# Causal attention in 32-row groups: scores and row maxima of one head each, from unmasked keys, with all masks on VectorE

## What is computed

```python
qkv = x @ W_qkv.T + b_qkv                     # x: layer norm of 4 x 1024 x 128
Q, K, V = ...                                 # each split into 16 heads of 8 channels
scores = jnp.einsum('bqhd,bkhd->bhqk', Q, K)
scores = jnp.where(causal, scores, -jnp.inf)
probs = jax.nn.softmax(scores / sqrt(hd), axis=-1)
out = jnp.einsum('bkhd,bhqk->bqhd', V, probs)
return out.reshape(B, S, H) @ W_o.T + b_o
```

## Time and profile before

| | |
|---|---|
| median of three runs | 2132.38 us |
| profiled execution | 2132.39 us, its span 2130.6 us |
| PE busy | 1859.3 us, 87% |
| DVE, ACT, POOL busy | 72%, 62%, 52% |
| scores L2207 | 768 matmuls, 226.3 us busy |
| maxima L2277, reductions L2419, masked maxima L2415 | 250.5, 230.9 and 157.3 us busy |
| values L2224 | 1536 matmuls, 164.1 us busy |
| head-mask products L2124 on POOL | 30, 108.0 us busy |

### The profile page before, as it was taken

The page is one execution under the profiler, slowest core; times in us unless marked ns, Lnnn a source line. Parts: engine busy times, 40 slices in busy tenths (PEclk is TensorE's granted clock), DMA queues, the critical chain, the costliest instruction groups (busy, mean ns, idle before and its releaser), DMA issues. The chain is left out here.

```text
span 2130.6 us, 30582 instructions
## 1 busy us (share of the span) xinstructions
PE 1859.3 (87%) x9650; PEld 1284.4 (60%) x9650; DVE 1538.1 (72%) x4002; ACT 1318.5 (62%) x2323; POOL 1114.9 (52%) x1073
## 2 busy tenths in 40 slices
PE   6887699997999966673799979999999999988999
PEld 3554588876788632332588845555555555547887
DVE  6996877756677679998677667766766766736775
ACT  3443388862788744442688845665666666557887
POOL 1110388862788822320688944543543543327888
PEclk8998799999899987876799989999999999998999
DMA  3000254400543300000333300000000000004442
GB/s 103 6 5 5 75 207 160 181 34 1 203 171 150 116 1 1 1 0 0 150 150 150 150 0 1 1 1 1 1 1 1 1 1 1 1 1 164 189 191 95
DMA packets 38803, 142.28 MB, mean 67 GB/s; under 512 B 6962, under 2 KB 18930, under 8 KB 26355
## 3 DMA queue, kind: packets, MB, share of 16 engines
q1 hardware_dynamic: 36336, 139.55, 16.9%
q10 hardware_dynamic: 2306, 0.78, 0.2%
HBM read 136.38 MB, written 3.93 MB: 66 GB/s over the span
## 5 line engine op out<-in xcount | busy, mean ns | idle before, releaser
L2327 ACT ACTIVATE soft_prob<-psum 128x1024 f32<-128x1024 f32 (+3 forms) x384 | 302.7, 813 | 205.5 <-PE psum L2207 203.9
L2419 DVE TENSOR_REDUCE soft_mx<-psum 128x1 f32<-128x512 f32 (+2 forms) x352 | 230.9, 687 | 116.5 <-PE psum L2277 79.4
L2277 PE MATMUL psum<-soft_own,soft_stack 128*128 128x512 f32 (+3 forms) x768 | 250.5, 378 | 24.1 <-DVE soft_mx L2415 10.5
L2207 PE MATMUL psum<-soft_stack,soft_own 128*128 128x512 f32 (+3 forms) x768 | 226.3, 378 | 2.7 <-POOL soft_stack L2184 2.2
L163 POOL TENSOR_TENSOR norm_rstd<-norm_mv,s_const_minus_half 128x4 f32<-128x4 f32 x64 | 65.5, 1023 | 275.9 <-DVE norm_mv L158 269.6
L2190 POOL TENSOR_SCALAR_AFFINE_SELECT soft_prob<-soft_prob 128x256 f32<-128x256 f32 x256 | 103.0, 409 | 203.6 <-ACT soft_prob L2327 200.8
L2207 PEld LDWEIGHTS psum<-soft_stack,soft_own 128*128 128x128 f32 x768 | 125.7, 190 | 133.3 <-issue 78.3
L2415 DVE CUSTOM_DVE_ANT_0 psum<-psum,s_soft_sel 128x384 f32<-128x384 f32 (+1 forms) x256 | 157.3, 639 | 66.2 <-PE psum L2277 65.5
L2277 PEld LDWEIGHTS psum<-soft_own,soft_stack 128*128 128x128 f32 x768 | 140.7, 194 | 92.5 <-DVE soft_mx L2419 42.8
L934 POOL TENSOR_TENSOR ffn0b_h_low<-ffn0b_t,ffn0b_h_high 128x512 fp32r<-128x512 f32 x128 | 162.3, 1297 | 29.9 <-ACT ffn0b_t L1067 29.8
L934 POOL TENSOR_TENSOR ffn1a_h_low<-ffn1a_t,ffn1a_h_high 128x512 fp32r<-128x512 f32 x128 | 162.3, 1300 | 27.5 <-ACT ffn1a_t L1067 26.9
(11 more groups left out here) (444 smaller groups left out, 5043.0 us busy)
## 6 DMA issues: line engine op xcount, KB each, us to landing
ffn0a_cw_all<-ffn0a_cw_dram SPq DMA_DIRECT2D x23, 1024.0 KB, 7.2
ffn0b_cw_all<-ffn0b_cw_dram SPq DMA_DIRECT2D x23, 1024.0 KB, 6.9
ffn1a_cw_all<-ffn1a_cw_dram SPq DMA_DIRECT2D x23, 1024.0 KB, 7.0
ffn1b_cw_all<-ffn1b_cw_dram SPq DMA_DIRECT2D x23, 1024.0 KB, 6.9
ffn0a_cw_all<-ffn0a_cw_dram SPq DMA_DIRECT2D x8, 768.0 KB, 10.9
ffn0b_cw_all<-ffn0b_cw_dram SPq DMA_DIRECT2D x8, 768.0 KB, 10.2
ffn1a_cw_all<-ffn1a_cw_dram SPq DMA_DIRECT2D x8, 768.0 KB, 10.4
ffn1b_cw_all<-ffn1b_cw_dram SPq DMA_DIRECT2D x8, 768.0 KB, 10.6
```

The source lines that it names most:

```text
L2207: ins = pe.matmul(e_ps[:, n % 2, j, low(n):BLK], own[:, u % 3, 2 * pair + j, kt * P:(kt + 1) * P], stack[:, u % HT, qb * BLK + low(n):(qb ...
L2277: ins = pe.matmul(per_head[:, n, :], stack[:, u % HT, i * P:(i + 1) * P], own[:, u % 3, g, half * BLK:half * BLK + width], start=(n == 0), ...
L2327: nc.scalar.activation(prob[:, done % PROBS, :, low(n):BLK], e_ps[:, n % 2, :, low(n):BLK], ACT.Exp, scale=float(HD) ** -0.5).then_inc(exp ...
L2419: nc.vector.tensor_reduce(mx[:, i, half, heads.start:heads.stop], bank[:, 0:width * len(heads)].rearrange("p (g k) -> p g k", k=width), AX ...
```

## The change

`own`, `ident`, `causal` and the event `own` are gone. `keys` has a slot for each of the four groups of heads. Scores and maxima take the 32 partitions of their head from `keys` and `stack` (`rows(g)`), so a matmul contracts 32 rows. Every maximum job is one head: 48 jobs a unit, in an order in which the two jobs of a step belong to the two heads that the step's scores don't use; all 32 jobs with the diagonal in them go through the custom instruction on DVE, the 16 others are reductions of 512. Jobs stand two to a step. In the start POOL writes the mask row ahead of the value pads.

```diff
 def max_jobs():
-    jobs = []
-    for i in range(TPB):
-        for half in range(1 + i // GT):
-            width = min(BLK, (i + 1) * P - half * BLK)
-            heads = BLK // width
-            jobs += [(i, half, width, range(g, g + heads)) for g in range(0, HT, heads)]
-    return jobs
+    order = (3, 0, 2, 1)
+    first = [(order[k ^ r], 0, (order[k ^ r] + 1) * P, (k + 2) % HT) for r in range(HT) for k in range(HT)]
+    second = []
+    for r in range(2 * HT):
+        for k in range(HT):
+            i, half = GT + order[k ^ (r // 2)], (k + r) % 2
+            second.append((i, half, (i + 1) * P - BLK if half else BLK, (k + 2) % HT))
+    return first + second
...
-            slots = [n for n in range(E_STEPS) for _ in range(2 if n % 2 or n % 8 == 0 else 1)]
             for j in range(M_JOBS):
-                at[slots[j * len(slots) // M_JOBS]].append(("m", u + 1, j))
+                at[j * E_STEPS // M_JOBS].append(("m", u + 1, j))
...
-        if u + 2 < UNITS:
-            put((9, ("own", u + 2, 0)), (16, ("own", u + 2, 1)))
...
-        keys = sb("keys", [P, 2, SEQ], F32R)
+        keys = sb("keys", [P, HT, SEQ], F32R)
...
-        own = sb("own", [P, 3, HT, SEQ], F32R)
...
+        def rows(g):
+            return slice(VW * g, VW * (g + 1))
...
                 for j in range(2):
-                    ins = pe.matmul(e_ps[:, n % 2, j, low(n):BLK], own[:, u % 3, 2 * pair + j, kt * P:(kt + 1) * P],
-                                    stack[:, u % HT, qb * BLK + low(n):(qb + 1) * BLK], start=True, stop=True)
+                    head = rows(2 * pair + j)
+                    ins = pe.matmul(e_ps[:, n % 2, j, low(n):BLK], keys[head, u % HT, kt * P:(kt + 1) * P],
+                                    stack[head, u % HT, qb * BLK + low(n):(qb + 1) * BLK], start=True, stop=True)
...
-                    for n, g in enumerate(heads):
-                        ins = pe.matmul(per_head[:, n, :], stack[:, u % HT, i * P:(i + 1) * P],
-                                        own[:, u % 3, g, half * BLK:half * BLK + width],
-                                        start=(n == 0), stop=half != i // GT or len(heads) == 1)
-                    if half == i // GT and len(heads) > 1:
-                        ins = pe.matmul(per_head[:, :, width - P:width], ident[:, :],
-                                        causal[:, :].unsqueeze(1).to_broadcast([P, len(heads), P]),
-                                        start=False, stop=True)
-                    ins.then_inc(m_ready, 1)
+                    pe.matmul(bank[:, 0:width], stack[rows(g), u % HT, i * P:(i + 1) * P],
+                              keys[rows(g), u % HT, half * BLK:half * BLK + width], start=True, stop=True)\
+                        .then_inc(m_ready, 1)
...
-                    if half == i // GT and len(heads) == 1:
+                    if half == i // GT:
```

More of the change, by code:

```diff
@@ L1980, in softmax_events @@
     start = [("pad", 0), ("stat", 1), ("scale", 1), ("qk", 0, 1), ("qk", 0, 0)]
-    start += [first[0], ("own", 0, 0), ("v", 0), first[1]]
-    start += [("xt", 1)] + maxima(0, 4) + [("qk", 1, 1)] + maxima(4, 8) + [("qk", 1, 0)] + maxima(8, M_FIRST)
-    start += [first[2], ("v", 1), second[0], ("sh", 0, 0), first[3], ("own", 0, 1)]
+    start += [first[0], ("v", 0), first[1]]
+    start += [("xt", 1)] + maxima(0, 6) + [("qk", 1, 1)] + maxima(6, 11) + [("qk", 1, 0)] + maxima(11, M_FIRST)
+    start += [first[2], ("v", 1), second[0], ("sh", 0, 0), first[3]]
     units = []
@@ L1999, in softmax_events @@
                 at[FIRST_STEPS + (j - 6) * (E_STEPS - FIRST_STEPS) // (M_JOBS - 6)].append(("m", 1, j))
[L2000 removed]
+            put(*zip((1, 3, 4), second[1:]))
             put((5, ("bias", 0)), (6, ("bias", 1)))
             put((9, ("oev", 0, 0)), *zip((10, 11, 13, 14), stack_events(0, 2)), (12, ("otr", 0, 0)), (15, ("sh", 1, 0)),
[L2003 removed]
+                *zip((17, 18, 20, 21), stack_events(0, 3)), (19, ("pad", 1)))
             units.append(at)
@@ L2158, in event @@
                         nc.gpsimd.tensor_copy(mask_row[:, BLK - P:BLK], w["causal"][:, :]).then_inc(mask_ready, 1)
[L2159 to L2164, removed]
-                        own_rows(nc.gpsimd, u, p, own_ready)
+                    nc.gpsimd.memset(v_pad[:, h, :, :, HD + 1:VW], 0.0)
+                    nc.gpsimd.memset(v_pad[:, h, :, :, HD:HD + 1], 1.0).then_inc(ones_set, 1)
                 if kind == "stat":
@@ L2265, in event @@
                     u, j = at
-                    i, half, width, heads = MJOBS[j]
+                    i, half, width, g = MJOBS[j]
                     bank, back = m_bank(u, j)
@@ L2345, in event @@
                     u, now = HT * b + t, slice(p * BLK, (p + 1) * BLK)
-                    if i == 0 and b > 0:
+                    if b > 0:
                         act.wait_ge(score_ready, E_STEPS * (u - HT + 1))
-                    if i == 1 and u >= 2:
-                        act.wait_ge(*((own_first, 2) if u == 2 else (own_ready, 2 * (u - 2))))
-                    nc.scalar.activation(stack[:, t, now] if i == 0 else keys[:, u % 2, now], ps[:, :, :], ACT.Identity,
+                    nc.scalar.activation(stack[:, t, now] if i == 0 else keys[:, t, now], ps[:, :, :], ACT.Identity,
                                          bias=w["shift_rows"][:, i:i + 1]).then_inc(used, 1)
@@ L2401, in event @@
                                             .to_broadcast(heads), ALU.add).then_inc(used_by("v", q), 1)
-                if kind == "own" and at[0] == 0:
-                    u, p = at
-                    dve.wait_ge(*freed("st", 0, 0, 1, p))
-                    own_rows(nc.vector, u, p, own_first)
                 if kind == "m":
                     u, j = at
-                    i, half, width, heads = MJOBS[j]
+                    i, half, width, g = MJOBS[j]
                     bank, _ = m_bank(u, j)
@@ L2416, in event @@
                                                        1.0, -3.0e38, ALU.add, ALU.max,
-                                                       mx[:, i, half, heads.start:heads.stop]).then_inc(m_done, 1)
+                                                       mx[:, i, half, g:g + 1]).then_inc(m_done, 1)
                     else:
-                        nc.vector.tensor_reduce(mx[:, i, half, heads.start:heads.stop],
-                                                bank[:, 0:width * len(heads)].rearrange("p (g k) -> p g k", k=width),
-                                                AX.X, ALU.max).then_inc(m_done, 1)
+                        nc.vector.tensor_reduce(mx[:, i, half, g:g + 1], bank[:, 0:width], AX.X, ALU.max)\
+                            .then_inc(m_done, 1)
                     if j in (M_FIRST - 1, M_JOBS - 1):
```

10 lines of the change are left out of this document (1 added, 9 removed).

## The result

The changed kernel took 2261.62 us (median of four runs, 2255.02 to 2267.20), the kernel before beside it 2132.44 us: a ratio of 1.0604 (95% interval 1.0575 to 1.0634), 129 us slower. The profiled execution has a span of 2260.0 us. Times here are medians; one of e10's four executions, at 3536 us, is out of line with the other three and is left out of its ratio.

The account below looks back on a forecast made before the run. PE's in-order chain, with waits for DVE to free banks, was taken as the bound: 2132.4 - 28 (units 1 to 14) + 1.5 (start) + 3 (unit 0) - 1.5 (unit 15) = 2107 us; range 2080 to 2160.

Parts of the forecast that it names:

- Row groups overlap: Four 32-row scores and maxima of a step run side by side; first maximum 0.2 us behind the first score.
- Rival (1): Scores and maxima: row groups don't overlap, first maximum over 0.35 us behind; unit 40.9 us, total 2152 us; chance 0.14.
- The start: Before unit 0: POOL's mask row ahead of the value pads and longer first maxima cost +1.2 to +2, taken +1.5 us.
- The steady unit, 38.0 us: Units 1 to 14: chain summed to 38.0 us against 39.8; gain taken as 2.0 a unit, 28 us in all.
- m0 to DVE: In each pair, from a step's first maximum on PE to DVE's start on it: 0.43 us, 5.2 a unit.
- The jobs: Units 1 to 14: 48 maxima jobs instead of 38, four a pair through two banks, DVE's first two jobs in the chain.
- Rival (2): Units 1 to 14: granted clock falls as overlap leaves PE less filled; a third of pairs +1.3 us, 2180 us; chance 0.09.
- Unit 0: First unit, 80 jobs instead of 65 through two banks: +3 us (-3 to +6) on 62.3.
- the prediction's sign: Unit 0 longer than 70 us would mean the two banks, not PE's stream, were always the link.
- Unit 15: Last unit, without maxima: faster scores, ACT takes over as limit; -1.5 us on 24.8.
- Rival (3): Around projections and transposes, 11 events a unit pay 0.2 to 0.4 us for shape changes; +45 us at worst; chance 0.08.

Follow-up runs that it names:

- e10: Changed kernel plus four extra 128-row matmuls of all 512 columns ahead of each odd step's scores; 2217 us, ratio 1.040.
- e1: Changed kernel plus two extra 128-row matmuls ahead of each odd step's scores, in the scores' own columns and banks; 2231 us, ratio 1.039.
- e2: Changed kernel plus four extra 32-row matmuls ahead of each odd step's scores, overlapping two by two; 2242 us, ratio 1.052.
- e3: Changed kernel with the two maxima of a step taken from the heads of its own scores; 2383 us, ratio 1.118.
- e5: Changed kernel with all scores and maxima from the first head's 32 rows, one row group, so no overlap; 2518 us, ratio 1.181.
- e6: Changed kernel plus two zero-weight 128-row, 512-column matmuls behind the scores of each step with the values' bank open; 2434 us, ratio 1.137.
- e7: Kernel before with only the scores from 32 rows; its 38 jobs, masks and 128-row maxima kept; 2153 us, ratio 1.010.
- e11: Kernel before plus one zero-weight 128-row, 512-column matmul a step in unit 0, where the values' bank is open; 2132.33 us, ratio 1.0003.
- e12: Kernel before plus two zero-weight 128-row, 512-column matmuls a step in unit 0, where the values' bank is open; 2137.77 us, ratio 1.0032.
- e4: Kernel before with the change's 48 one-head jobs, masks on DVE and two jobs a step, but 128 rows of masked keys; 2199 us, ratio 1.032.
- e9: Kernel before, its 38 jobs and masked keys kept, with 64 rows for scores and for one- and two-head maxima; 2180 us, ratio 1.021.
- e8: Kernel before with the 48-job list, masks on DVE and 128-row scores, but maxima from 32 rows; 2350 us, ratio 1.105.

## Why the prediction was wrong, step by step

- **Row groups overlap: right, and better than taken.** In nine of ten pairs the first maximum starts with the first score (0.01 us), not 0.2 behind. Rival (1)'s condition, 0.35, held in three of 168 pairs, where PE waited for a bank.
- **The start: +1.6 us against +1.5, which may be chance.** Runs with the changed kernel's start (e1, e2, e3, e5, e6, e10) begin unit 0 between 1258.9 and 1262.2 us, those with the start of before (e7, e11, e12) between 1258.5 and 1260.8.
- **The steady unit, 38.0 us: the sum was for a clock that was not granted.** This is the step that failed. The other terms came out nearly right: 62 of the 168 pairs of steps of units 1 to 14 (starts of even steps' scores to the next) lie wholly at 2.4 GHz, from ten of the twelve places that a pair can have in a unit. They are on average 0.08 us shorter than the same pairs of the same units before, 0.9 us a unit; averaged place by place it is 1.35 us in those ten. So at full clock the unit would be some 38.5 to 39 us, a gain of about 1 where 2.0 were forecast. In the pair shown, one term that grew is m0 to DVE: 0.52 (1569.96 to 1570.48) instead of 0.43.
- **The jobs: a little over the forecast.** The unit without any overlap was put at 40.9 us in rival (1), 1.1 over before. e4 measured 44.1, but its four units without the collision are 1.6 to 2.2 over. From there to about 1 below before, overlap and narrow shapes give some 3 us back, as the 2.9 forecast (40.9 to 38.0).
- **Rival (2), the clock, is what happened, with 0.09.** Its reason was half wrong and its share too small. It said that overlap leaves less of the unit filled; e5 shows a full PE with 32 rows at 1.2 GHz. It was argued away by unit 15, which kept 2.4 GHz. But that unit kept it with 128-row scores; after, with PE busy 28.57 of 29.86 us, the same unit ran at 0.61. Its price for a pair was near: it took +1.3 us, and 68 pairs wholly at 1.2 GHz are on average 1.10 us longer than the same pairs of before. But it asked for a third of the pairs; the mean of 0.71 means half clock for 58% of the time, and another 38 pairs have it in part (0.87 us longer each).
- **Unit 0: +19.2 instead of +3.** e4 gave 70.6 us, +8.3, of which 1.8 is a wait behind the collision; the rest, for jobs through two banks, is just over the top of -3 to +6. The other 10.9 came with the clock's fall from 0.86 to 0.59. e7, with the job list of before, has 72.2 us at 0.67, so a unit 0 of over 70 us doesn't by itself point to the banks, as the prediction's sign had it. **Unit 15: +5.1 instead of -1.5**, with the clock at 0.61; in e9 with 64 rows it kept 2.4 GHz and is 1.6 us shorter than before, to the end of its last values.
- **Rival (3), changes of shape**, was taken to matter around 11 events. e7 shows it at full clock between scores and whatever has another shape. The Trainium skill (TensorEngine Tiling (Array Packing), Key Properties) says that a change of tiling mode drains TensorE; the runs agree and put it near 0.2 us.

The whole, against the kernel before: in units 1 to 14 the 62 pairs at 2.4 GHz give 4.8 us, the 68 at 1.2 GHz cost 74.8 and the 38 with both levels 32.9, together the 102.9; unit 0 adds 19.2, unit 15 5.1, the start 1.6.

What stays open: the worth of the change at full clock, known only from pairs and from units with added work; whether the extra rows could be put where they cost nothing; whether it is the number of rows or the way that a part of the rows is addressed that the clock answers to (64 rows in e9 kept it in nine of 14 units); and how rows and waits add up. e7 and e8 have the same columns from 32 rows and from 128 (18,432 of each a unit, scores and maxima exchanged, e7's mask matmuls aside), yet the clock was 1.00 in one and 0.81 in the other, so the share of rows does not settle it alone.

## What to carry to other kernels

Packing small contractions into row groups shortens TensorE's streams and may take its clock, and then the untouched full-height matmuls pay: before such a change, ask what fraction of the array's rows the rest of the stage keeps at work, not how busy the engine looks. A busy share of 0.99 says nothing on that. Splitting packed jobs into one job per head to make them fit costs a bank, a semaphore and a fixed part of DVE's time for each (here some 2 us a unit for ten more jobs), so cost the job list alone first, and look in the trace of such a control for waits that neither of the two kernels has; and keep all that changes shape together, since a change took about 0.2 us here.

## What the hardware showed that I had not expected

- Granted clock 0.56 with PE busy 99% of 902 us, from matmuls of 32 rows in one group; 0.98 with the same streams from 128 rows, whose few falls come with or right behind a wait of some 2.5 us (e5, e4).
- Adding work made the kernel faster: four 128-row matmuls in each pair took units 1 to 14 from 47.2 to 42.6 us (e10).
- Four 32-row matmuls into four banks begin within 0.01 us of each other, and the next scores 0.29 us later (two scores of 384 columns, maxima of 384 and 512; the changed kernel). Two overlapped scores of 512 columns hold PE for 0.43 us until a 128-row matmul starts (e7).
- A DVE operation on 16 elements a partition took 0.18 us alone and 2.8 to 3.5 us each of the eleven times that a 3.6 us product of POOL ran beside it (e4).
